# Cross-attention kernel: output projection in fp16 pairs from the second tile on, with the weight work replanned

## What is computed

```python
q = _split_heads(hidden_states @ Wq.T, H)
k = _split_heads(text @ Wk.T, H)
v = _split_heads(text @ Wv.T, H)
out_text = _merge_heads(_attend(q, k, v, sm_scale))   # softmax(q k^T * sm_scale) v
...
out = out @ Wo.T + bo
return out + residual
```

## Time and profile before

| | |
|---|---|
| median of 3 runs | 427.18 us (426.95 to 427.48) |
| profiled execution | 427.04 us |
| its span, first to last instruction | 425.2 us |
| TensorE busy | 416.9 us, 98% |
| GpSimd busy | 306.2 us, 72% |
| ScalarE busy | 301.0 us, 71% |
| DVE busy | 263.1 us, 62% |
| mean granted TensorE clock | 0.999 |

### The profile page before, as it was taken

The page is one execution under the profiler, slowest core; times in us unless marked ns, Lnnn a source line. Parts: engine busy times, 40 slices in busy tenths (PEclk is TensorE's granted clock), DMA queues, the critical chain, the costliest instruction groups (busy, mean ns, idle before and its releaser), DMA issues.

```text
span 425.2 us, 8268 instructions
## 1 busy us (share of the span) xinstructions
PE 416.9 (98%) x2550; PEld 238.9 (56%) x2550; DVE 263.1 (62%) x544; ACT 301.0 (71%) x584; POOL 306.2 (72%) x267
## 2 busy tenths in 40 slices
PE   8999999999999999999999999999999999999996
PEld 6877775677777755544444444444444444444442
DVE  0354676755676687776677656765677655556723
ACT  1638888857477788998767975888667966966720
POOL 8327799999659698798959594769649594764560
PEclk9999999999999999999999999999999999999999
DMA  8997636444844576454753347334743446345203
GB/s 270 371 345 244 229 114 217 158 155 145 280 156 156 186 259 207 158 169 143 257 184 125 134 149 243 126 135 174 248 166 127 148 150 222 132 167 192 84 25 125
DMA packets 41781, 77.33 MB, mean 182 GB/s; under 512 B 5264, under 2 KB 6416, under 8 KB 41744
## 3 DMA queue, kind: packets, MB, share of 16 engines
q1 hardware_dynamic: 30944, 57.21, 38.7%
q10 hardware_dynamic: 10800, 19.67, 14.3%
HBM read 33.40 MB, written 10.49 MB: 103 GB/s over the span
## 4 chain that ended last, share of the span: by engine, by line
PE 86%; ACT 3%; DMA 2%; issue 2%; DVE 2%; SPq 2%; POOL 1%; ACTq 0%; DVEq 0%; POOLq 0%
PE ps_q L928 28%; PE ps_o L928 27%; PE ps_s L993 9%; PE ps_pv L1000 7%; PE ps_m L979 5%; PE ps_den L1005 4%; PE ps_o L900 2%; DMA x_f<-in_x 2%; PE ps_m L1050 1%; PE ps_m L984 1%; SPq L367 1%; PE ps_q L1050 1%; PE ps_s L1050 1%; PE ps_o L1050 1%; ACT p_hi L584 1%
## 5 line engine op out<-in xcount | busy, mean ns | idle before, releaser
L449 POOL TENSOR_TENSOR p_lo<-p_f,p_hi 77x512 f16<-77x512 f32 x160 | 183.2, 1165 | 85.9 <-ACT p_hi L584 84.7
L580 ACT ACTIVATE p_f<-ps_s 77x512 f32<-77x512 f32 x160 | 94.3, 589 | 21.8 <-PE ps_s L993 20.7
L716 DVE TENSOR_REDUCE mx<-ps_m 128x4 f32<-128x308 f32 x160 | 69.2, 475 | 44.5 <-PE ps_m L979 43.6
L584 ACT ACTIVATE p_hi<-ps_s 77x512 f16<-77x512 f32 x160 | 93.5, 584 | 2.5 <-PE ps_den L1005 2.4
L928 PE MATMUL ps_o<-attn,wo 128*128 128x512 f16 x360 | 90.0, 381 | 0.4 <-DVE sums L791 0.2
L928 PE MATMUL ps_q<-x,wq 128*128 128x512 f16 x375 | 85.1, 379 | 0.0
L993 PE MATMUL ps_s<-q_packed,k_packed 128*77 128x512 f32 x160 | 63.4, 439 | 0.3
L928 PEld LDWEIGHTS ps_q<-x,wq 128*128 128x128 f16 x375 | 36.3, 98 | 44.5 <-issue 0.8
L928 PEld LDWEIGHTS ps_o<-attn,wo 128*128 128x128 f16 x360 | 31.2, 98 | 38.1 <-issue 6.6
L705 DVE SCALAR_TENSOR_TENSOR q_lo<-ps_q,q_scale,q_hi 128x512 fp32r<-128x512 f32 x25 | 18.8, 751 | 49.6 <-ACT q_hi L563 49.6
L979 PE MATMUL ps_m<-k_diag,q_hi 128*128 128x308 f32 x160 | 42.3, 344 | 0.6 <-ACT q_hi L563 0.6
(11 more groups left out here) (126 smaller groups left out, 661.9 us busy)
## 6 DMA issues: line engine op xcount, KB each, us to landing
q_packed<-q_hi SPq DMA_DIRECT2D x80, 256.0 KB, 2.5
x_f<-in_x SPq DMA_DIRECT2D x45, 256.0 KB, 4.3
q_packed<-q_lo SPq DMA_DIRECT2D x40, 256.0 KB, 3.3
x_res<-in_x ACTq DMA_DIRECT2D x35, 256.0 KB, 2.7
out<-x_res ACTq DMA_DIRECT2D x35, 256.0 KB, 2.7
wq_sb<-in_wq SPq DMA_DIRECT2D x10, 320.0 KB, 4.2
wo_sb<-in_wo SPq DMA_DIRECT2D x10, 320.0 KB, 4.0
wk_sb<-in_wk SPq DMA_DIRECT2D x8, 320.0 KB, 5.5
```

The lines of the kernel that those rows point to most:

```text
L449: nc.gpsimd.tensor_tensor(p_lo[:, i, :], p_f[:, i, :], p_hi[:, i, :], ALU.subtract).then_inc(plo_done, 1)
L580: nc.scalar.activation(p_f[:, i, :], ps_s[i % 2][0:L, :], ACT.Exp, scale=SCALE).then_inc(pf_done, 1)
L584: nc.scalar.activation(p_hi[:, i, :], ps_s[i % 2][0:L, :], ACT.Exp, scale=SCALE).then_inc(phi_done, 1)
L716: nc.vector.tensor_reduce(mx[:, g % RS, :, tt], ps_m[tt % 2][:, 0:HG * L].rearrange("p (h k) -> p h k", k=L), AX_X, ALU.max).then_inc(max_ ...
```

## The change

The output projection uses fp16 pairs from tile 1 on instead of tile 2. For that, `Wo` is loaded again in steps 7 to 11 and its tops, high and low halves come earlier. The query weights keep their second load (steps 9 to 13), but their tops, high and low halves are spread differently. The scale sums run in steps 6 to 16 instead of 10 to 18. What stands below is the diff with its tables whole.

```diff
-    FIRST_Q16, FIRST_O16 = 3, 2
+    FIRST_Q16, FIRST_O16, FIRST_SUM = 3, 1, 6
...
     def wo_again_at(t, g):
-        return planned({12: (0,), 13: (1,), 14: (2,), 15: (3,), 16: (4,)}, t, g)
+        return planned({7: (0,), 8: (1,), 9: (2,), 10: (3,), 11: (4,)}, t, g)
...
     def wq_top_at(t, g):
-        return planned({9: (0,), 11: (1,), 12: (2,), 13: (3, 4)}, t, g)
+        return planned({10: (0,), 11: (1,), 12: (2,), 13: (3,), 14: (4,)}, t, g)
 
     def wo_top_at(t, g):
-        return planned({12: (0,), 13: (1,), 14: (2,), 16: (3,), 17: (4,)}, t, g)
+        return planned({7: (0,), 8: (1,), 9: (2,), 12: (3,), 13: (4,)}, t, g)
 
     def is_v_top(t, g):
-        return isinstance(t, int) and (t, g) == (1, G - 1)
+        return isinstance(t, int) and nth(t, g) == FIRST_SUM - 1
 
     def has_sums(t, g):
 
         if isinstance(t, int) and t < 4:
-            return 2 * G <= nth(t, g) < 4 * G - 1
+            return FIRST_SUM <= nth(t, g) <= 3 * G + 1
         return g == 1 and has_next(t)
...
     def wq_half_high_at(t, g):
-        return planned({10: (0,), 12: (1,), 13: (2,), 14: (3, 4)}, t, g)
+        return planned({12: (0,), 13: (1,), 14: (2,), 15: (3,), 16: (4,)}, t, g)
 
     def wo_half_high_at(t, g):
-        return planned({13: (0,), 14: (1,), 15: (2,), 17: (3,), 18: (4,)}, t, g)
+        return planned({8: (0,), 9: (1,), 10: (2,), 13: (3,), 14: (4,)}, t, g)
 
     def wq_half_low_at(t, g):
-        return planned({11: (0,), 13: (1, 2), 14: (3, 4)}, t, g)
+        return planned({13: (0,), 14: (1, 2), 16: (3, 4)}, t, g)
 
     def wo_half_low_at(t, g):
-        return planned({13: (0,), 16: (1, 2), 18: (3, 4)}, t, g)
+        return planned({9: (0, 1), 11: (2,), 13: (3,), 14: (4,)}, t, g)
...
             def set_q_scale(t, g):
...
-                    dve.wait_ge(w_scales, {0: 1, 1: 2, 2: 3, 3: 5, 4: 6}[g])
+                    dve.wait_ge(w_scales, {0: 4, 1: 5, 2: 6, 3: 8, 4: 10}[g])
...
             def sum_tops(t, g):
 
                 pe.wait_ge(tops_done, tops_before(t, g))
-                if isinstance(t, int) and nth(t, g) == 2 * G:
+                if isinstance(t, int) and nth(t, g) == FIRST_SUM:
                     pe.wait_ge(down_done, 2)
-                pe.wait_ge(outs_done, nth(*out_tiles(t, g)[0]))
+                else:
+                    pe.wait_ge(outs_done, nth(*out_tiles(t, g)[0]))
```

More of the change, by code:

```diff
@@ L153, in tops_before @@
         total = 0
-        for n in range(2 * G - 1, nth(t, g)):
+        for n in range(FIRST_SUM - 1, nth(t, g)):
             at = n // G, n % G
-            total += len(x_tops_at(*at)[1]) + len(wq_top_at(*at)) + len(wo_top_at(*at)) + is_v_top(*at)
+            xt, chunks = x_tops_at(*at)
+            total += len(chunks) if x_in_half(xt) else 0
+            total += len(wq_top_at(*at)) + len(wo_top_at(*at)) + is_v_top(*at)
         return total
     def sums_so_far(t, g):
-        return nth(t, g) - 2 * G + 1 if isinstance(t, int) and t < 4 else 2 * G - 1 + t - 3
+        return nth(t, g) - FIRST_SUM + 1 if isinstance(t, int) and t < 4 else 3 * G + 2 - FIRST_SUM + t - 3
     def x_scaled_at(t, g):
```

## The result

Median 442.97 us (440.77 to 443.37, 4 runs) against 427.33 us before. The ratio is 1.036 (95% interval 1.034 to 1.037), slower. The profiled execution took 443.30 us, with a span of 441.5 us; that is 16.3 us over the profiled execution of before. The forecast was 437.1 us, its range ended at 440.5.

A forecast was written before the change was run, and what follows sets the result against it. The prediction took TensorE, busy for 98% of the span, to bound the kernel. Its terms, -1.0 + 0.7 - 1.5 + 11.9 = +10.1 us on 427.04, gave 437.1 us, 2.3% slower, range 434.8 to 440.5.

The forecast's parts named there:

- The waits: TensorE waits for GpSimd's Wq low halves before the query projections of steps 13, 14 and 16: +11.9 us together.
- The clock: Forecast: no slower clock priced. Rival: TensorE's clock falls in one or more waits, 438.9 us once, 442.5 thrice; chance 0.17.
- The rest: Everything but TensorE's waits: fp16 output -1.0, sums +0.7, ScalarE's lateness -1.5 us.
- four early sums: Steps 6 to 9 get one scale sum each at 0.28 us; less two dropped in steps 17 and 18, +0.7 us.
- The fp16 output: Output matmuls of tile 1, five groups in steps 11 to 15, 0.2 us less each: -1.0 us.
- ScalarE's late step: Step 14, where ScalarE prepares three groups, loses 1.14 us; after the change no step prepares more than two.
- two groups fit on ScalarE: Step 13's window is on time at 9.96 us with two groups prepared, so ScalarE's lateness should go: -1.5 us together.
- Not slower: Rival: GpSimd's weight groups are ready in time in steps 13, 14 and 16, no waits, 425.2 us; chance 0.04.
- Wo is late: Rival: Wo's loads or groups 3 and 4 come late, steps 11 to 15 wait, 438 to 440 us; chance 0.05.

The follow-up runs named there:

- the kernel with a single wait of 3.3 us: Low halves of Wq groups 1 and 2 moved from step 13 to step 14, in the kernel before the change: 430.67 us, ratio 1.007.

## Why the prediction was wrong

**The waits: right.** Steps 13, 14 and 16 and no others. 4.5, 3.5 and 3.9 us were read from the earlier trace rows. The idle times were 4.4, 3.3 and 3.8; the prediction counted from the start of the first matmul, and by that count 4.6, 3.5 and 3.9 came, 12.0 against 11.9. Steps 15 and 17 had none, and Wo was in time.

**The clock: the step that failed.** The sum priced it at nothing ("the forecast does not use it"), and its rival got 0.17, most of it for a single fall. It fell behind all three waits, 6.3 us. Two reasons show in the text. The argument against it was that no row shows a fall; but no row showed an idle stretch of 2 us either once TensorE had begun (the longest is 0.68 us), so this spoke for neither side. And the range took in one fall only, although the three waits are of one kind and would sooner fall together: the rival's own value for three, 442.5, is 0.5 us from the median. Its price of 1.8 us, from the warm-up row, was near two of the falls (1.7 each) and 1.1 below the third (2.9). The rule of the Trainium skill (TensorE: Matmul & The Clock Gate, "Part 1: The HAM clock gate") is that an idle array falls back to half its clock and gets it back by working. The trace agrees: 0.50 behind the waits, and 1.00 again by 163.6, 181.0 and 204.5. Filling the waits with work settles it. What stays open is why one fall of the same kernel lasts longer than another, and why a like wait lets the clock fall in one execution and not in the next.

**The rest: right in sum, with two terms off that partly cancel.** Expected -1.8 us, measured -2.0 (1.3 less 3.3). The windows with four early sums grew by 0.3 each, 1.3, where 1.1 was priced. The fp16 output gave 1.4, not 1.0: the earlier trace rows shows one of the three pieces of a group, and in the first piece of a step with a sum the gain is twice as large. In step 12 the chain has 1.53, 1.36 and 0.70 us for the pieces before, and 1.37, 1.31 and 0.65 after. ScalarE's late step gave its 1.1, and steps 17 and 18 their 0.7, as priced. But what was read from step 13, that two groups fit on ScalarE, does not carry over to step 16: its `q_high` is late with one group, and in the changed kernel only TensorE's wait there hid it. Without the falls the profiled execution would stand at 443.3 - 6.3 = 437.0 us; the forecast was 437.1. A last slip is small: by its own numbers the wait of step 14 is 168.09 - 164.53 = 3.6, not 3.5.

**The rivals.** "Not slower" asked for the weight group ahead of the four `p_low`; the kernel that does just that takes 426.2 us where 425.2 was worked out; TensorE's waits for `p_low` and for ScalarE's late `q_high`, 0.27 and 0.74 us, stand in the difference. "Wo is late" did not happen here, but did with the old plan of Wq beside the new one of Wo.

## What to carry to other kernels

When one engine prepares what another consumes in the same step, compare two instants in the trace: when the preparer reaches that item in its list, and when the consumer arrives. The number of steps or the share of busy time says nothing; here 1.4 us of work, at the wrong end of a list on an engine busy for 72%, cost some 4 us three times over, and at the head of the list 0.27 us of idle time. If a change opens idle stretches of some microseconds on TensorE, price a slower clock behind each of them as the likely case, and all of them together, not one. And a load taken off one late step of a nearly full engine must be followed to the step that receives it.

## What the runs showed of the hardware

The granted clock fell behind idle stretches of TensorE of 4.4, 3.8 and 3.3 us, and also behind 2.4 and 2.0 us; behind one of 1.7 us it did not, in two traces. It is no fixed matter: the kernel with a single wait of 3.3 us ran once in four at full clock (429.2 against 430.5 to 431.4 us). A fall cost 1.3 to 2.9 us in the 15 matmuls behind it (4.72 to 6.33 us against 3.41), while the idle stretch before it can still read 1.00. And matmuls on constant data in a wait, which compute nothing, made the changed kernel 6.4 us faster.
